# Making u\*B of three state indices with ScalarE and TensorE in a selective scan, and loading C in thirds

## The chip, the cores and the metric

The kernel runs on one core of one Trainium2 chip. The metric is the time of one execution on the device, in microseconds, median over the runs. Engines are named as in the profile: PE (TensorE, matrix products and transposes), DVE (VectorE), ACT (ScalarE), POOL (GpSimd), SP (SyncE, which only issues DMAs here).

## What is computed

One decoder layer over x of shape (4, 1024, 256) in fp32: a Mamba block, cross attention on 154 context tokens, and a mixture of four experts, each with a residual and a layer norm behind it. The change lies in the Mamba block:

```python
xz = x @ W_in.T
x_ssm, z = split(xz, 2)                        # 512 channels each
x_ssm = silu(causal_conv4(x_ssm) + conv_b)
proj = x_ssm @ W_x.T                           # B: 16, C: 16, dt: 1
dt = softplus(proj[..., -1:] * W_dt[:, 0] + b_dt)
def step(h, (dt_t, Bt, Ct, xt)):               # h: (batch, 512, 16)
    h = exp(dt_t[..., None] * A) * h + (xt * dt_t)[..., None] * Bt[:, None, :]
    y = einsum('bdn,bn->bd', h, Ct)
y = (y + x_ssm * D_param) * silu(z)
out = y @ W_out.T
```

With u = x\*dt, the term added in each step of the recurrence is u\*B of the state index n.

## The kernel before, in words

`mamba_block` (from L45) runs first, over all tokens; `attn_ffn_block` (L771) follows and isn't touched. The 4096 tokens are 16 chunks of 256 (TC), four to a batch entry. A turn i works through the 16 state indices of chunk i; beside that it prepares chunk i+1 (`prepare`), finishes the output of chunk i-1 (`finish`) and the layer norm of chunk i-2 (`settle`). Channels lie on the partitions, 512 channels as 4 groups (CT) of 128; tokens run along the free dimension.

For a state index n (a step):
- PE broadcasts row n of B to all partitions, into one of two PSUM banks `b_ps` (`b_row`, L332, run two steps ahead: PE slot n makes row n+2).
- DVE multiplies u by it, two channel groups at a time (h = 0, 1), into one of three PSUM banks `bu_ps` (`make_bu`, L677, 128x512); adds what is carried over from the chunk before to the first column (`add_carry`, L691; not in the first chunk of a batch entry); and scans (`scans`, L704, 128x512) into a ring of four `state` buffers. The order on DVE is written out in `step` (L715): make_bu(n,1), scans(n,0), add_carry(n,1), make_bu(n+1,0), scans(n,1), add_carry(n+1,0).
- ACT makes `decay` = exp(dt\*A) of step n, four instructions of 128x255, also in a ring of four, so that it can be up to four steps ahead of the scans (`step`, L482).
- POOL multiplies the state by C broadcast over the partitions (`c_bc`), 128x1024, into `state_c` (L635). A scan of step n waits for the product of step n-4.
- PE adds eight 128x128 blocks of `state_c`, transposed against the identity, to `y_ps` (`add_state`, L339, two slots behind).

All five engines run their instructions strictly in the order written here; `turn` of each engine has a list of (slot, work), and the work of slot n follows the instructions of step n. The slots of the preparation of chunk k = i+1 are, before the change: PE convolutions 0, 1, 3, 4, z tiles 5, 6, `project` 8, `step_row` 9; ACT `take_conv` 4, 7, `take_z` 8, 9, `silus` 10, `copies` 11, `terms` and `softplus` 12, `next_lead` 13; POOL `split` 8, 10, `make_dt` 10, `make_u` 11. Then come the pieces of the other chunks: PE `y_back` 11, 12 and `out_tile` 13, 14 (chunk i-1); ACT `take_sum` 0, 1, `guess` 5, `normalise` 9 (chunk i-2), `take_y_back` 14, 15 (chunk i-1); POOL `variance` 2 and `newton` 4. `take_y` on DVE stands in step 2. All matrix results of the preparation and of the output pass through one PSUM bank, `w_ps`, one after the other.

`load_c` on SP (L205) waits for `proj`, stores the rows of C of chunk k to DRAM, and loads them back broadcast over the partitions, in two halves of 8 rows; the second buffer of `c_bc` holds the other chunk. The load waits for `take_y` of the chunk that used the buffer.

Of the kernel before, what the change touches and what calls it, by code (L numbers as in the profile page):

```python
# [8 lines left out]
ALU = mybir.AluOpType  # L9
# [35 lines left out]
def mamba_block(nc, x, xT, w_in, cw, w_x, w_out, par, ident_sb, ident, sel_bc, sel_p, c_dram, x1, ahead, s_ahead):  # L45
# [7 lines left out]
    with ExitStack() as ctx:  # L53
# [8 lines left out]
        SKIP_AT = 8  # L62

# [12 lines left out]
        relu = sb("relu", [P, CT, TC])  # L76
# [48 lines left out]
        s_cb = [[sem(f"s_cb{q}{h}") for h in range(2)] for q in range(2)]  # L125
# [64 lines left out]

        block = ctx.enter_context(nc.Block())

        @block.sync
        def _(sp):
# [10 lines left out]
            def load_c(k):  # L205
# [5 lines left out]
                sp.wait_ge(s_y, count)  # L211
                for h in range(2):
                    n = NS // 2
                    sp.dma_start(c_bc[:, q, h * n:(h + 1) * n, :],
                                 c_dram[bass.ds(at(k, NS, h * n), n), :].partition_broadcast(P)).then_inc(s_cb[q][h], 16)
# [42 lines left out]
        def _(pe):  # L258
            def conv(k, j):

                q, first = k[1] % 2, k[1] % CPB == 0
                if j == 0:
                    pe.wait_ge(s_xT[q], loads(k))
                    if not is_first(k):
                        pe.wait_ge(s_abs, at(k, 2 * CT, 0))
                        pe.wait_ge(s_r, at(k, CTT, 0))
# [33 lines left out]
            def step_row(k):  # L300
                pe.wait_ge(s_projc, at(k, 2, 2))
                nc.tensor.matmul(w_ps[:, 0:TC], sel_p_sb[:, :], proj[:, k[1] % 2, :], start=True, stop=True)\
                  .then_inc(s_step, 1)

            def y_back(k, t):
                if t == 0:
                    more = k[0] is not None or k[1] + 2 < NCH
                    pe.wait_ge(s_y, at(k, 16, 48))
                    pe.wait_ge(s_abs, at(k, 2 * CT, 6 * CT) if more else 2 * CT * NCH)
                    if not more:  # L310
                        pe.wait_ge(s_r, at(k, CTT, 2 * CTT))
# [46 lines left out]
            def turn(i, prepare, finish, settle):  # L358
                k, last = shift(i, 1), shift(i, -1)
                work = []  # L360
                if prepare:
                    work += [(0, lambda: conv(k, 0)), (1, lambda: conv(k, 1)), (3, lambda: conv(k, 2)),
                             (4, lambda: conv(k, 3)), (5, lambda: z_tile(k, 0)), (6, lambda: z_tile(k, 1)),
                             (8, lambda: project(k)), (9, lambda: step_row(k))]
# [3 lines left out]
                for n in range(NS):  # L368
# [8 lines left out]
                    for place, what in work:  # L377
                        if place == n:
# [26 lines left out]
        def _(act):  # L405
# [38 lines left out]
            def terms(k, j):  # L444
                if j == 0:
# [3 lines left out]
                nc.scalar.activation(relu[:, j, :], w_ps[:, 0:TC], ACT.Relu,  # L449
                                     scale=col("W_dt", j), bias=col("b_dt", j)).then_inc(s_abs, 1)  # L450

# [1282 lines left out]
```

## Time and profile before

| | us |
|---|---|
| median of 3 runs | 1843.66 (1841.05 to 1845.77) |
| profiled execution, its time | 1843.35 |
| its span, first to last instruction | 1841.6 |
| busy PE / DVE / ACT / POOL over the span | 1483.1 / 1431.3 / 1110.4 / 919.3 |
| mean granted clock of PE | 0.895 of full |
| first and last scan (L711) start | 55.5 / 996.4 |

Busy time is the union of the intervals of an engine's instructions. Instructions of one engine overlap a little at their ends, so a pitch, from start to start, is shorter than a duration. Rows with [x <-ENGINE tile line] say that the engine stood idle for x us before the instruction and what released it.

### The profile page before, as it was taken

The numbers are of one execution on the slowest core, as the hardware profiler recorded it, in microseconds if no ns is written. First come the engines' busy times: TensorE is split into PE (matmuls) and PEld (weight loads), VectorE is DVE, ScalarE is ACT, GpSimd is POOL, SyncE is SP. The second block draws the span as 40 slices with busy tenths as digits, with TensorE's granted clock in tenths as the row PEclk, the third lists the DMA queues.
The fourth block names the chain that finished last, engine by engine and source line by source line (L and its number), as shares of the span: only waits on it lengthen the run. The fifth ranks groups of instructions, "written<-read, shape, count | busy, mean of one in ns | idle before, by whom it ended". The sixth has DMA issues, their size and how long they took to land. (4 is left out here: it accounts for less than half of the span.)

```text
span 1841.6 us, 23560 instructions
## 1 busy us (share of the span) xinstructions
PE 1483.1 (81%) x7984; PEld 1050.1 (57%) x7984; DVE 1431.3 (78%) x2667; ACT 1110.4 (60%) x2370; POOL 919.3 (50%) x758
## 2 busy tenths in 40 slices
PE   4777888777887888877866679988998899889880
PEld 3566667666776667765755345555545545464470
DVE  1899999999999999999997244395449654964578
ACT  2767877688667876787673224347634763376471
POOL 0687778877787778787785100004500460036005
PEclk9888899998898898889966879999999999999895
DMA  3311110111011110111010301000010001000000
GB/s 119 129 52 52 64 52 12 64 64 64 6 59 64 64 53 13 64 64 58 1 62 13 127 1 42 9 1 1 13 61 1 1 1 46 1 1 1 23 1 23
DMA packets 38331, 71.19 MB, mean 39 GB/s; under 512 B 3585, under 2 KB 31842, under 8 KB 33858
## 3 DMA queue, kind: packets, MB, share of 16 engines
q1 hardware_dynamic: 38210, 69.68, 11.1%
q8 instruction: 63, 1.03, 0.2%
q14 instruction: 58, 0.48, 0.1%
HBM read 61.02 MB, written 8.65 MB: 38 GB/s over the span
## 5 line engine op out<-in xcount | busy, mean ns | idle before, releaser
L635 POOL TENSOR_TENSOR state_c<-state,c_bc 128x1024 f32<-128x1024 f32 x256 | 601.5, 2361 | 127.1 <-DVE state L711 98.3
L711 DVE TENSOR_TENSOR_SCAN state<-decay,bu_ps 128x512 f32<-128x512 f32 x512 | 620.3, 1211 | 0.2 <-ACT decay L491 0.2
L491 ACT ACTIVATE decay<-dt_sb,negA 128x255 f32<-128x255 f32 x1024 | 432.4, 496 | 0.0
L686 DVE TENSOR_TENSOR bu_ps<-u_sb,b_ps 128x512 f32<-128x512 f32 x512 | 349.7, 683 | 50.6 <-POOL u_sb L556 37.4
L1330 POOL TENSOR_TENSOR big<-big,g_sb 128x1024 f32<-128x1024 f32 x29 | 79.2, 2733 | 619.0 <-ACT big L1215 617.7
L352 PE MATMUL y_ps<-ident_sb,state_c 128*128 128x128 f32 x2048 | 297.2, 293 | 18.1 <-POOL state_c L635 17.3
L352 PEld LDWEIGHTS y_ps<-ident_sb,state_c 128*128 128x128 f32 x2048 | 256.7, 152 | 53.3 <-POOL state_c L635 33.1
L273 PE MATMUL w_ps<-xT_sb,w_conv 128*128 128x256 f32 (+1 forms) x1024 | 237.1, 385 | 13.6 <-DVE w_conv L754 12.7
L273 PEld LDWEIGHTS w_ps<-xT_sb,w_conv 128*128 128x128 f32 x1024 | 193.1, 194 | 39.8 <-DVE w_conv L754 12.7
L336 PE MATMUL b_ps<-parts,sel_bc_sb 96*128 96x256 bf16 x256 | 75.7, 296 | 98.1 <-DVE bu_ps L702 74.9
L1398 DVE TENSOR_REDUCE neg<-ps 128x8 f32<-128x1232 f32 x64 | 91.0, 1436 | 69.7 <-PE ps L1009 69.7
L1129 PE MATMUL ps<-w_sb,x1T_sb 128*128 128x512 f32 x256 | 130.6, 649 | 0.0
L1164 PE MATMUL ps<-w_sb,hT 128*128 128x256 f32 x512 | 119.1, 386 | 2.4 <-ACT hT L1288 1.9
L1422 DVE BATCH_NORM_STATS2 stats<-big 128x6 f32<-128x256 f32 x256 | 88.2, 411 | 30.0 <-ACT big L1293 19.1
L412 ACT ACTIVATE xs<-w_ps,par_sb 128x256 f32<-128x256 f32 x64 | 26.8, 470 | 138.2 <-PE w_ps L273 138.2
L1164 PEld LDWEIGHTS ps<-w_sb,hT 128*128 128x128 f32 x512 | 96.0, 193 | 18.8 <-ACT hT L1288 5.1
L1273 ACT ACTIVATE big<-ps 128x1024 f32<-128x1024 f32 x32 | 32.8, 1024 | 119.5 <-PE ps L1129 119.5
L336 PEld LDWEIGHTS b_ps<-parts,sel_bc_sb 96*128 96x128 bf16 x256 | 26.2, 103 | 128.7 <-DVE bu_ps L702 93.0
L1334 POOL TENSOR_TENSOR acc<-acc,big 128x256 f32<-128x256 f32 x116 | 89.8, 774 | 9.1
L1225 ACT ACTIVATE hT<-ps 128x1024 f32<-128x1024 f32 x64 | 61.5, 1011 | 53.3 <-PE ps L1046 53.3
L1129 PEld LDWEIGHTS ps<-w_sb,x1T_sb 128*128 128x128 f32 x256 | 48.9, 205 | 52.5 <-issue 52.5
L1501 DVE COPY raw<-ps 128x512 f32<-128x512 f32 x32 | 22.1, 692 | 70.2 <-PE ps L1060 69.6
(160 smaller groups left out, 2406.6 us busy)
## 6 DMA issues: line engine op xcount, KB each, us to landing
c_bc<-c_scratch SPq DMA_DIRECT2D x32, 1024.0 KB, 5.9
res<-in_x SPq DMA_DIRECT2D x16, 256.0 KB, 2.8
x_scratch<-res SPq DMA_DIRECT2D x16, 256.0 KB, 7.5
stage<-x_scratch SPq DMA_DIRECT2D x4, 1024.0 KB, 7.1
xa<-x_scratch SPq DMA_DIRECT2D x4, 1024.0 KB, 6.2
out_x<-acc SPq DMA_DIRECT2D x4, 1024.0 KB, 4.4
xT_sb<-in_xT SPq DMA_DIRECT2D x12, 259.0 KB, 3.4
w_sb<-in_w SPq DMA_DIRECT2D x2, 1024.0 KB, 12.7
```

Of the source, the lines that this page charges most:

```text
L273: last = nc.tensor.matmul(w_ps[:, at_col + skip:at_col + TC], w_conv[:, TAPS - 1 - back, c, j * P:(j + 1) * P], xT_sb[:, q, c, HALO + skip ...
L336: nc.tensor.matmul(b_ps[n % 2][:, 0:TC], sel_bc_sb[:, n, :], parts[:, i[1] % 2, :], start=True, stop=True)\
L352: last = nc.tensor.matmul(y_ps[:, t * DI + j * P:t * DI + (j + 1) * P], state_c[:, n % RING, j, t * P:(t + 1) * P], ident_sb[:, :], start= ...
L491: nc.scalar.activation(decay[:, n % RING, j, 1:], dt_sb[:, i[1] % 2, j, 1:], ACT.Exp, scale=negA[:, j * NS + n:j * NS + n + 1]).then_inc(s ...
L635: nc.gpsimd.tensor_tensor(state_c[:, n % RING, :, :], state[:, n % RING, :, :], c_bc[:, q, n, :].unsqueeze(1).to_broadcast([P, CT, TC]), A ...
L686: nc.vector.tensor_tensor(bu_ps[m % 3][:, :].rearrange("p (j n) -> p j n", j=2), u_sb[:, i[1] % 2, 2 * h:2 * h + 2, :], b_ps[n % 2][:, 0:T ...
L711: nc.vector.tensor_tensor_scan(state[:, n % RING, pair, :].rearrange("p j n -> p (j n)"), decay[:, n % RING, pair, :].rearrange("p j n -> ...
L1129: last = nc.tensor.matmul(dst, xT[:, k, t * P:(t + 1) * P], w1_sb[:, k, h * HALF:(h + 1) * HALF], start=False, stop=k == KT - 1, skip_grou ...
L1164: last = nc.tensor.matmul(dst, hT[:, e * KT + k, i * P:(i + 1) * P], w2_sb[:, e * KT + k, :], start=False, stop=k == KT - 1, skip_group_ch ...
L1334: nc.gpsimd.tensor_tensor(acc[:, t, :], acc[:, t, :], tile[:, e * DM:(e + 1) * DM], ALU.add).then_inc(s_sum, 1)
L1398: nc.vector.tensor_reduce(neg[:, u:u + 2, :].rearrange("p m (j c) -> p j m c", c=BLK)[:, :, :, HD], ps[:, base:base + HG, 0:2 * S].rearran ...
L1422: nc.vector.bn_stats(stats[:, i * E + e, :], big[:, n, i, e * DM:(e + 1) * DM]).then_inc(s_st, 1)
```

## The change

For the state indices `OFF = (6, 10, 14)` DVE no longer makes u\*B. Instead PE transposes u to token-major (`turn_u`, 8 transposes a turn, through `w_ps`), ACT copies it to SBUF (`take_u`), and for each of the three indices ACT scales it by B, which is a per-partition scalar in that layout (`scale_u`, two activations of 128x512, each), and PE transposes the product back into PSUM (`fill`, two times four transposes), the first half into the `b_ps` bank of that index, where no row is broadcast then, the second into a `bu_ps` bank. B in token-major form comes out of `step_row` by two more transposes and is copied by `take_bT`. The Relu of `terms` goes into `u_sb` instead of a buffer of its own, and `c_bc` has three buffers of 8 rows instead of four halves; a load waits for the POOL products that read the buffer last. Slots of the preparation move: PE convolutions 2, 3, 4, 5, z 6, 7, `project` 9, `step_row` 10; ACT `take_conv` 6, 8, `take_z` 9, 10, `copies` 12, `terms`, `softplus` and `next_lead` 13; POOL's slots stay.

```diff
+        OFF = (6, 10, 14)
+        K = len(OFF)
...
-        c_bc = sb("c_bc", [P, 2, NS, TC])
+        c_bc = sb("c_bc", [P, 3, NS // 2, TC])
+        uT_sb = sb("uT_sb", [P, CTT, DI])
+        uB = sb("uB", [P, 2, CTT, DI])
+        bT = sb("bT", [P, 2, CTT, NS])
...
+        def place(i, n, h):
+            if n in OFF and h == 0:
+                return b_ps[n % 2]
+            return bu_ps[use(i, n, h) % 3]
...
-                sp.wait_ge(s_y, count)
                 for h in range(2):
...
+                    part = 2 * k[1] + h
+                    if part >= 3:
+                        sp.wait_ge(s_sc, RING + (part - 2) * n)
...
                     if not is_first(k):
-                        pe.wait_ge(s_abs, at(k, 2 * CT, 0))
-                        pe.wait_ge(s_r, at(k, CTT, 0))
+                        pe.wait_ge(s_uTc, at(k, CTT, 0))
...
+            def turn_u(i, t):
+
+                if t == 0:
+                    pe.wait_ge(s_u, at(i, 1, 1))
+                    pe.wait_ge(s_abs, at(i, 2 * CT, 2 * CT))
+                    pe.wait_ge(s_bT, at(i, 1, 1))
+                    pe.wait_ge(s_r, at(i, CTT, CTT))
+                else:
+                    pe.wait_ge(s_uTc, at(i, CTT, t))
...
+            def b_free(i, n):
...
+                before = (i, n - 2) if n >= 2 else (shift(i, -1), n - 2 + NS)
+                if before[1] in OFF:
+                    pe.wait_ge(s_scan, scanned(before[0][1], before[1], 0))
+                else:
+                    pe.wait_ge(s_bu, multiplied(*before, 1))
+
+            def fill(i, n, h):
+
+                if h == 0:
+                    b_free(i, n)
+                    pe.wait_ge(s_uB, CTT * (i[1] * K + OFF.index(n) + 1))
+                else:
+                    pe.wait_ge(s_scan, freed(i, n, 1))
+                dst, slot = place(i, n, h), (i[1] * K + OFF.index(n)) % 2
+                for e in range(2):
+                    for t in range(CTT):
+                        j = 2 * h + e
+                        last = nc.tensor.transpose(dst[:, e * TC + t * P:e * TC + (t + 1) * P],
+                                                   uB[:, slot, t, j * P:(j + 1) * P], ident_sb[:, :])
+                last.then_inc(s_fill, 1)
...
             def b_row(i, n):
+                if n in OFF:
+                    fill(i, n, 0)
+                    return
...
-                pe.wait_ge(s_bu, at(i, 4 * NS, 4 * n + 4))
+                b_free(i, n)
...
+                    if n + 1 in OFF:
+                        fill(i, n + 1, 1)
...
+            def scale_u(i, n):
+
+                o = i[1] * K + OFF.index(n)
+                act.wait_ge(s_uTc, at(i, CTT, CTT))
+                act.wait_ge(s_bT, at(i, 1, 1))
+                if o >= 2:
+                    act.wait_ge(s_fill, 2 * (o - 1))
+                for t in range(CTT):
+                    nc.scalar.activation(uB[:, o % 2, t, :], uT_sb[:, t, :], ACT.Copy,
+                                         scale=bT[:, i[1] % 2, t, n:n + 1]).then_inc(s_uB, 1)
...
+                work += [(3, lambda: take_u(i, 0)), (4, lambda: take_u(i, 1))]
                 if prepare:
...
+                    work += [(6, lambda: take_conv(k, 0)), (8, lambda: take_conv(k, 1)), (9, lambda: take_z(k, 0)),
+                             (10, lambda: take_z(k, 1)), (10, lambda: silus(k)), (12, lambda: copies(k)),
+                             (13, lambda: terms(k, 0)), (13, lambda: take_bT(k)), (13, lambda: terms(k, 1)),
+                             (13, lambda: terms(k, 2)), (13, lambda: terms(k, 3)), (13, lambda: softplus(k)),
                              (13, lambda: next_lead(k))]
+                work += [(n - 1, lambda n=n: scale_u(i, n)) for n in OFF]
...
             def make_bu(i, n, h):
 
-                m = 2 * n + h
-                if m == 0:
+                if n in OFF:
+                    return
...
+            def made(i, n, h):
+                if n in OFF:
+                    dve.wait_ge(s_fill, filled(i, n, h))
+                else:
+                    dve.wait_ge(s_bu, multiplied(i, n, h))
...
+                if more:
+                    make_bu(*following, 0)
+                    if following[1] in OFF:
+                        add_carry(*following, 0)
                 between(4 * n + 2)
                 scans(i, n, 1)
...
+                if more and following[1] not in OFF:
+                    add_carry(*following, 0)
```

## Rows read from the trace of the kernel before

**Rows 1.** Page, part 2: DVE's busy tenths in 40 slices

```profile
DVE  1899999999999999999997244395449654964578
```

**Rows 2.** Windows, turns 1-14: length, PE/PEld/DVE/ACT/POOL busy, PEclk, DMA, GB/s

```profile
110.60:940.00 829.40, 679.92 (x3777) 554.21 (x3778) 816.26 (x1289) 619.32 (x1557) 651.21 (x513) 0.90 0.14 49
```

**Rows 3.** Lines, same window: xcount | busy, mean ns | idle before, releaser

```profile
L491 ACT ACTIVATE decay<-dt_sb,negA 128x255 f32<-128x255 f32 x892 | 377.0, 496 | 0.0
...
L412 ACT ACTIVATE xs<-w_ps,par_sb 128x256 f32<-128x256 f32 x56 | 23.5, 470 | 111.7 <-PE w_ps L273 111.7
```

**Rows 4.** Timeline, DVE: start, length, engine, line, operation, tiles, xcount

```profile
110.61 1.22 DVE L711 TENSOR_TENSOR_SCAN state<-decay,bu_ps 128x512 f32<-128x512 f32 x1
...
345.00 1.21 DVE L711 TENSOR_TENSOR_SCAN state<-decay,bu_ps 128x512 f32<-128x512 f32 x1
...
353.94 1.21 DVE L669 TENSOR_TENSOR yg<-y_ps,gate 128x1024 f32<-128x1024 f32 x1
355.07 0.68 DVE L686 TENSOR_TENSOR bu_ps<-u_sb,b_ps 128x512 f32<-128x512 f32 x1
355.66 1.21 DVE L711 TENSOR_TENSOR_SCAN state<-decay,bu_ps 128x512 f32<-128x512 f32 x1
356.79 0.15 DVE L702 TENSOR_TENSOR bu_ps<-bu_ps,inject 128x2 f32<-128x2 f32 x1
356.84 0.68 DVE L686 TENSOR_TENSOR bu_ps<-u_sb,b_ps 128x512 f32<-128x512 f32 x1
357.44 1.21 DVE L711 TENSOR_TENSOR_SCAN state<-decay,bu_ps 128x512 f32<-128x512 f32 x1
...
400.04 1.21 DVE L711 TENSOR_TENSOR_SCAN state<-decay,bu_ps 128x512 f32<-128x512 f32 x1
...
403.84 1.21 DVE L711 TENSOR_TENSOR_SCAN state<-decay,bu_ps 128x512 f32<-128x512 f32 x1
...
940.02 1.21 DVE L711 TENSOR_TENSOR_SCAN state<-decay,bu_ps 128x512 f32<-128x512 f32 x1
```

**Rows 5.** Timeline of PE, turn 5

```profile
348.01 3.62 PE L273 MATMUL w_ps<-xT_sb,w_conv 128*128 128x256 f32 x16
...
364.21 3.62 PE L273 MATMUL w_ps<-xT_sb,w_conv 128*128 128x256 f32 x16
...
385.76 1.04 PE L352 MATMUL y_ps<-ident_sb,state_c 128*128 128x128 f32 x8
...
388.74 0.63 PE L315 MATMUL w_ps<-ident_sb,yg 128*128 128x128 f32 x4 [0.40 <-ACT relu L449]
...
396.68 1.97 PE L352 MATMUL y_ps<-ident_sb,state_c 128*128 128x128 f32 x8 [0.49 <-POOL state_c L635]
```

**Rows 6.** Lines, whole span, ACT: forms nearest to a scaling

```profile
L1288 ACT ACTIVATE hT<-ps,lnp_sb 128x512 f32<-128x512 f32 x64 | 45.4, 772 | 8.8 <-PE ps L1150 8.8
...
L1249 ACT ACTIVATE lnd<-lnd 128x512 f32<-128x512 f32 x32 | 20.2, 630 | 1.0
```

**Rows 7.** Part 6 of the page, DMA issues: the loads of C

```profile
c_bc<-c_scratch SPq DMA_DIRECT2D x32, 1024.0 KB, 5.9
```

**Rows 8.** Timeline of ACT, turn 5

```profile
361.07 0.20 ACT L478 ACTIVATE lnv<-var 128x2 f32<-128x2 f32 x1 [2.43 <-POOL var L603]
...
367.87 0.84 ACT L412 ACTIVATE xs<-w_ps,par_sb 128x256 f32<-128x256 f32 x2 [2.98 <-PE w_ps L273]
...
390.77 1.69 ACT L491 ACTIVATE decay<-dt_sb,negA 128x255 f32<-128x255 f32 x4
392.37 0.49 ACT L441 ACTIVATE lead<-rest,par_sb 96x256 bf16<-96x256 f32 x1
392.76 0.19 ACT L489 ACTIVATE carry<-state 128x4 f32<-128x4 f32 x1
```

**Rows 9.** Timeline of POOL, turn 5

```profile
390.85 2.36 POOL L551 TENSOR_TENSOR dt_sb<-dt_sb,relu 128x1024 f32<-128x1024 f32 x1 [2.19 <-ACT dt_sb L457]
...
394.28 2.35 POOL L635 TENSOR_TENSOR state_c<-state,c_bc 128x1024 f32<-128x1024 f32 x1
```

More of the change, by code:

```diff
@@ L62, in mamba_block @@
         SKIP_AT = 8
+        OFF = (6, 10, 14)
+        K = len(OFF)
+        USES = [(n, h) for n in range(NS) for h in range(2) if n not in OFF or h == 1]
+        PROD = [(n, h) for n in range(NS) for h in range(2) if n not in OFF]
         w_conv = sb("w_conv", [P, TAPS, KT, DI])
@@ L189, in turns, with use, scanned, freed @@
                 turn((None, r), prepare=r + 1 < NCH, finish=r >= 1, settle=r >= 2)
+        def use(i, n, h):
+            return i[1] * len(USES) + USES.index((n, h))
+        def place(i, n, h):
+            if n in OFF and h == 0:
+                return b_ps[n % 2]
+            return bu_ps[use(i, n, h) % 3]
+        def scanned(r, n, h):
+            return 2 * RING + r * 2 * NS + 2 * n + h + 1
+        def freed(i, n, h):
+            before = use(i, n, h) - 3
+            if before < 0:
+                return 0
+            return scanned(before // len(USES), *USES[before % len(USES)])
+        def multiplied(i, n, h):
+            return i[1] * len(PROD) + PROD.index((n, h)) + 1
+        def filled(i, n, h):
+            return 2 * (i[1] * K + OFF.index(n)) + h + 1
+        def broadcast(i, n):
+            return i[1] * (NS - K) + sum(m not in OFF for m in range(n + 1))
+        def added(i, n, h):
+            return (i[1] - i[1] // CPB - 1) * 2 * NS + 2 * n + h + 1
         block = ctx.enter_context(nc.Block())
@@ L376, in turn @@
                         add_state(last, NS + n - LAG)
-                    for place, what in work:
-                        if place == n:
+                    if n + 1 in OFF:
+                        fill(i, n + 1, 1)
+                    for slot, what in work:
+                        if slot == n:
                             what()
@@ L448, in terms, with take_bT, take_u @@
                                      scale=col("W_dt", j), bias=col("b_dt", j)).then_inc(s_abs, 1)
-                nc.scalar.activation(relu[:, j, :], w_ps[:, 0:TC], ACT.Relu,
+                nc.scalar.activation(u_sb[:, k[1] % 2, j, :], w_ps[:, 0:TC], ACT.Relu,
                                      scale=col("W_dt", j), bias=col("b_dt", j)).then_inc(s_abs, 1)
+            def take_bT(k):
+                if k[1] >= 2:
+                    act.wait_ge(s_uB, CTT * K * (k[1] - 1))
+                nc.scalar.activation(bT[:, k[1] % 2, :, :].rearrange("p t n -> p (t n)"),
+                                     w_ps[:, TC:TC + CTT * NS], ACT.Copy).then_inc(s_bT, 1)
+            def take_u(i, t):
+                act.wait_ge(s_uT, at(i, CTT, t + 1))
+                if t == 0 and i[1]:
+                    act.wait_ge(s_uB, CTT * K * i[1])
+                nc.scalar.activation(uT_sb[:, t, :], w_ps[:, :], ACT.Copy).then_inc(s_uTc, 1)
+            def scale_u(i, n):
[4 more added lines that the diff above has]
+                    act.wait_ge(s_fill, 2 * (o - 1))
+                for t in range(CTT):
+                    nc.scalar.activation(uB[:, o % 2, t, :], uT_sb[:, t, :], ACT.Copy,
+                                         scale=bT[:, i[1] % 2, t, n:n + 1]).then_inc(s_uB, 1)
             def softplus(k):
@@ L529, in _ @@
                 terms(first, j)
+            take_bT(first)
             softplus(first)
@@ L620, in turn @@
             def turn(i, prepare, finish, settle):
-                k, old, q = shift(i, 1), shift(i, -2), i[1] % 2
+                k, old = shift(i, 1), shift(i, -2)
                 work = []
@@ L712, in scans @@
                                              decay[:, n % RING, pair, :].rearrange("p j n -> p (j n)"),
-                                             bu_ps[m % 3][:, :], 0.0, ALU.mult, ALU.add).then_inc(s_scan, 1)
+                                             place(i, n, h)[:, :], 0.0, ALU.mult, ALU.add).then_inc(s_scan, 1)
             def step(i, n, prepare, between):
+                following = (i, n + 1) if n + 1 < NS else (shift(i, 1), 0)
+                more = n + 1 < NS or prepare
                 make_bu(i, n, 1)
```

82 lines of the change are left out of this document (44 added, 38 removed).

## The prediction

> **What bounds the kernel now.** The page comes first: VectorE (DVE) is nearly full over the first 22 of 40 slices, the Mamba stage, and half empty after it [rows 1]. The change touches only that stage. The window of its 14 middle turns (one turn is one chunk of 256 tokens) shows DVE busy for 816 of 829 us, with TensorE (PE) at 680, ScalarE (ACT) at 619 and GpSimd (POOL) at 651 [rows 2]. So DVE sets the pace and every other engine has room on average. An average hides order, however. ACT's room is time spent standing in front of a named result, 111.7 us of it for the convolutions alone [rows 3]: room that lies at a few places in the turn and is of use only there.
>
> The DVE timeline gives the pace. A step n is two scans, two products bu = u\*B and two small carry additions. Start to start, a scan takes 1.13, an addition 0.05 and a product 0.59: 3.55 a step [rows 4]. I write times as + us from a turn's first scan; turn 5 starts at 345.00 and lasts 58.8, and the 14 middle turns last (940.02 - 110.61) / 14 = 59.2 on average [rows 4]. Scan (3,1st half) starts at 357.44, +12.4.
>
> **What DVE saves.** For n = 6, 10, 14 both products go: 6 x 0.59 = 3.6 a turn. In return scan (n-1,2nd) has only small additions between itself and the addition it reads, up to 0.1 each time, 0.3 a turn (bounds 0 and 3 x 0.15). Nothing else on DVE changes. If all the rest were hidden a turn would last 55.5.
>
> **What is added elsewhere.** PE: 8 transposes of u, 24 of the scaled u, 2 small ones, less 3 row broadcasts. Four transposes take 0.63 in one group and eight add-ups with their tail 1.04 at full clock, 1.97 at the lower one [rows 5]; I take 0.5 a group of four at full clock, 1.0 at low. That is 8 x 0.5 = 4 us of PE a turn. ACT: two copies of u out of PSUM and one of B, and 6 scalings of 128x512 with a per-partition scale. No row shows that form. A 512-wide activation within SBUF with a constant scale takes 630 ns, a 512-wide one from PSUM with scale and bias from SBUF 772 [rows 6]; I take the first, which shares the memory and the width, so 1.25 a pair, and keep 1.54 as the far end. The lower end is 1.16, if one overlaps the next by 0.1, as the decays do (four at 496 ns in 1.69 [rows 3, 8]). Loads of C: each half now waits for products of an older half instead of take_y; copies(k) comes about 45 us into the turn, and store plus load (5.9 us median for the load [rows 7]) end before +60, while the first product of the next turn begins past +68. I cost it at nothing; the load of residuals behind it on SP's queue is wanted a whole turn later. The Relu going straight into u_sb costs nothing, being the same instruction. One relief: row broadcasts wait for the product alone and no more for the carry addition, 1.2 us earlier.
>
> **What is moved, and where it ends.** This decides. The preparation of the next chunk is one chain through w_ps. Today its first convolution starts at 348.01, +3.0, its last starts at 364.21 and ends at +22.8; ACT takes it at 367.87, +22.9, and after decays, silus, copies, terms and softplus begins decay(13) at 390.77, +45.8 [rows 5, 8].
>
> After the change turn_u stands first in w_ps and conv(k,0) moves to PE slot 2. There it stands behind the broadcast for step 4, which waits for product (2,2nd), done at 12.4 - 3.55 - 1.13 (take_y, 353.94 to 355.07 [rows 4]) + 0.1 = +7.8, and behind add_state(0), 0.9 more: start at about +8.9. The second pair of convolutions waits for take_conv(k,0), now in ACT slot 6, behind guess (today at 361.07, +16.1, after a wait of 2.43 for POOL's variance [rows 8]), a pair of scalings 1.25, decay(6) 1.7 and its own 0.8: +19.9. Two convolutions at 3.45, their add_states and fill(6,1) take 9.0: the last ends near +28.9, 6 us later than today.
>
> From taking that result to the end of softplus ACT needs 22.9 today, with five steps of decays in it. It needs the same afterwards, less the 0.4 that it waits today, plus scale_u(10) 1.25 and take_bT 0.25: 24.0, so softplus ends at +52.9. In the same slot 13 follow next_lead (0.4 start to start [rows 8]) and, last, scale_u(14) 1.25: +54.6. fill(14,0) on PE ends at +55.1. DVE cannot start scan (14,1st) without it. It wants it at the end of scan (13,1st): scan 13 would start at 12.4 + 10 x 3.55 - 4 x 0.59 = +45.5 with no stall, so fill(14,0) is wanted at +46.7. It is 8.4 late. Part of that shows earlier: fill(6,1) comes at +25.3 for +23.0 (2.3), and decay(11) at +42 for +40.7 (1.2); the remaining 4.9 is at step 14. Together scan (14,1st) starts at 55.1 + 0.2 + 1.13 = +56.4.
>
> Then a second wait. fill(14,1) stands behind add_state(11), and POOL makes product 11 only after make_dt, which waits for softplus: from make_dt's start to product 11 is 394.28 - 390.85 = 3.4, and product 11 takes 2.35 [rows 9]. 52.9 + 5.8 + 0.9 + 0.5 = +60.1, wanted at 56.4 + 1.13: 2.6 late. From there the turn needs its 3.55 and the 3.8 of the last step (400.04 to 403.84 [rows 4]): 56.4 + 2.6 + 7.4 = +66.4. PE stands idle for about 3 us twice before these fills; today an idle wait of that kind comes before a stretch at the lower of the two clock levels (eight transposes in 1.97 at 396.68 [rows 5]). One add_state and one fill at that level cost 0.9 more: **67.3 a turn.**
>
> **Sum.** 14 turns x (67.3 - 59.2) = +113. Turn 0 has the same chain without normalise and guess and runs 55.1 today: +7. Turn 15 prepares nothing and keeps the saving, -3.6. Rounded, +117. The profiled execution took 1843.35, 0.3 under the median of 1843.66: 1843.35 + 117 = **1960**. Low end of this case: scalings at 1.16 a pair, no low clock, product 11 not late, and 1.2 us of the relief at the broadcasts reaching conv(k,0): 62.4 a turn, +48, 1891. High end: scalings at 1.54, fills, add_states and output tiles at the lower clock (+2.5): 70 a turn, +155, 1998.
>
> **Rivals.** (a) Faster. All the added work lies in the idle time of ACT and PE, and DVE keeps its saving: 14 x (59.2 - 55.5) + 2 x 3.5 = 59 less, 1785. For it: DVE is 98% busy and ACT idle for 210 of 829 us. It decides at one point: scale_u(14) has to end by +46.2 and by my count ends at +54.6. An error of 8 us in a chain of 46 that mostly repeats rows of today would be large; 9%. A middle case within 0.3% needs the chain 7 us shorter and just so; 2%. (b) The first wait alone: the order at fill(14,1) costs nothing because product 11 is done in time. 56.4 + 7.4 = 63.8 a turn, +68 with turns 0 and 15, 1911. POOL's strict order speaks against it; 12%. (c) Transposes slower than counted. The row has eight in 1.04 us at full clock and 1.97 at low [rows 5]. If every added group and the add_states beside it run at the low level, the path gains 0.5 for each of four groups and 0.9 for each of two add_states on top: 3.8 - 0.9 already counted = 2.9 a turn, +44, 2004; 4%, as PE stands at 0.90 of full clock over these turns [rows 2], most of them spent at the higher level. The Trainium skill (TensorE: Matmul & The Clock Gate, Part 4: PE-mode transpose) says a transpose took about 275 ns in a kernel and doesn't count as activity that keeps the clock at full. By that figure, an estimate, 34 transposes would cost 9 us of PE a turn in place of 4; eight in 1.04 us here disagree with the duration, and no row separates the clock part. My forecast holds 73%.
>
> **Numbers.** Cases (my forecast, b, c and part of the uncertainty of each) are slower: 89%. A measurement of this kernel tells 0.3%, 5.5 us, from no change. The range 1890 to 2000 holds the forecast's ends and (b).
>
> **What the new profile should show.** DVE busy in the middle turns near 85%, down from 98%, with idle before the carry addition L702 and the scan L711, released by PE's fills; some ACT-released idle at step 11. Mean turn near 67. ACT's scalings of about 0.63, the third pair ending near +54.6, directly after next_lead. conv(k,0) near +9. POOL waits longer for softplus. I am wrong if conv(k,0) starts before +5 or the third pair of scalings ends before +47, and the later stages should not move at all.

## The result, and the profile after

The changed kernel takes 1973.97 us in the median (1971.84 to 1977.89, 4 runs) against 1843.68 for the kernel before: a ratio of 1.071, 95% interval 1.0687 to 1.0733. Slower by 130 us, where 1960 was forecast.

The page after:

```profile
span 1976.1 us, 24624 instructions
...
PE 1561.1 (79%) x8480; PEld 1119.7 (57%) x8480; DVE 1383.0 (70%) x2571; ACT 1185.0 (60%) x2514; POOL 919.5 (47%) x758
...
DVE  1778888787878778787878915448555855674578
```

DVE lost 48 us of work (1431.3 to 1383.0) and the span grew by 134.5. Its row of tenths, full through the Mamba stage in [rows 1], now has sevens and eights in it. Where the time lies can be read from the first scans of the turns: 16 numbers from the trace of either kernel.

| | before | after | difference |
|---|---|---|---|
| start of the first scan | 55.5 | 58.6 | +3.1 |
| turn 0 | 55.1 | 64.6 | +9.5 |
| turns 1 to 14, mean of one | 59.24 | 68.21 | 14 x 8.97 = +125.6 |
| first to last scan of turn 15 | 56.3 | 53.0 | -3.3 |
| last scan to the end | 845.2 | 845.0 | -0.2 |

The windows view over the same 14 turns (length, then busy PE, PEld, DVE, ACT, POOL, clock, DMA) answers to [rows 2]:

```profile
123.20:1078.00 954.80, 752.32 (x4210) 619.02 (x4209) 774.32 (x1205) 684.78 (x1683) 650.48 (x512) 0.88 0.12 42
```

DVE falls from 98% to 81% of its turns. No engine has taken its place: PE is at 79%, ACT at 72%, POOL at 68%. So this is a chain of waits and not a full engine. The waits view of the same stretch (total us, times, longest) names its links:

```profile
POOL rest L699 <- ACT lead L524: 114.0, 14, 8.4
...
DVE b_ps L827 <- PE b_ps L386: 67.3, 22, 5.1
DVE bu_ps L827 <- PE bu_ps L386: 60.8, 22, 3.3
...
PE y_ps L442 <- DVE yg L788: 28.1, 14, 2.0
DVE state L838 <- ACT decay L606: 27.8, 17, 4.3
```

DVE stands 128 us for fills (L386), which did not exist before, and 28 us for ACT's decay. The timeline of DVE in turn 5, which now runs from 394.51 to 463.42, 68.9 us (columns as in [rows 4], the idle time and its releaser in brackets), gives each of them its place:

```profile
394.51 1.21 DVE L838 TENSOR_TENSOR_SCAN state<-decay,bu_ps 128x512 f32<-128x512 f32 x1
...
412.24 0.69 DVE L806 TENSOR_TENSOR bu_ps<-u_sb,b_ps 128x512 f32<-128x512 f32 x1 [0.36 <-PE b_ps L426]
...
417.01 0.17 DVE L827 TENSOR_TENSOR b_ps<-b_ps,inject 128x2 f32<-128x2 f32 x1 [1.11 <-PE b_ps L386]
...
422.77 0.17 DVE L827 TENSOR_TENSOR bu_ps<-bu_ps,inject 128x2 f32<-128x2 f32 x1 [3.35 <-PE bu_ps L386]
...
439.37 1.22 DVE L838 TENSOR_TENSOR_SCAN state<-decay,bu_ps 128x512 f32<-128x512 f32 x1 [0.97 <-ACT decay L606]
...
452.82 0.17 DVE L827 TENSOR_TENSOR b_ps<-b_ps,inject 128x2 f32<-128x2 f32 x1 [5.06 <-PE b_ps L386]
...
457.42 0.17 DVE L827 TENSOR_TENSOR bu_ps<-bu_ps,inject 128x2 f32<-128x2 f32 x1 [2.19 <-PE bu_ps L386]
...
463.42 1.21 DVE L838 TENSOR_TENSOR_SCAN state<-decay,bu_ps 128x512 f32<-128x512 f32 x1
```

These are the first halves and second halves of index 6 (417.01, 422.77) and of index 14 (452.82, 457.42); for index 10 DVE doesn't wait. 439.37 is the scan of step 11, behind ACT. Together with 0.36 us before the product at 412.24 this is 13.0 us of idle time in the turn. Minus the 3.6 that DVE saves it gives 9.4 of the 10.1 us by which turn 5 grew. The addition at 452.82 stands ahead of the second scan of step 13, which reads nothing of the fill and waits behind it all the same; the order with that scan (1.13 us) first was not tried.

### The profile page after: what moved, and what is told of

Same layout as the page of the kernel before. It is cut to its first block and busy times, and to the rows that moved or that the text cites. A ratio compares the mean times of both kernels' runs of the same rounds, so it can differ in the third digit from the quotient of the medians.

```text
span 1976.1 us, 24624 instructions
## 1 busy us (share of the span) xinstructions
PE 1561.1 (79%) x8480; PEld 1119.7 (57%) x8480; DVE 1383.0 (70%) x2571; ACT 1185.0 (60%) x2514; POOL 919.5 (47%) x758
## 5 line engine op out<-in xcount | busy, mean ns | idle before, releaser
L838 DVE TENSOR_TENSOR_SCAN state<-decay,bu_ps 128x512 f32<-128x512 f32 x464 | 561.5, 1212 | 26.6 <-ACT decay L606 16.1
L442 PE MATMUL y_ps<-ident_sb,state_c 128*128 128x128 f32 x2048 | 314.8, 305 | 94.4 <-POOL state_c L754 64.2
L442 PEld LDWEIGHTS y_ps<-ident_sb,state_c 128*128 128x128 f32 x2048 | 266.3, 158 | 130.0 <-POOL state_c L754 83.3
L806 DVE TENSOR_TENSOR bu_ps<-u_sb,b_ps 128x512 f32<-128x512 f32 x416 | 284.4, 684 | 60.9 <-POOL u_sb L674 40.0
L316 PE MATMUL w_ps<-xT_sb,w_conv 128*128 128x256 f32 (+1 forms) x1024 | 258.2, 410 | 13.6 <-DVE w_conv L880 12.6
L316 PEld LDWEIGHTS w_ps<-xT_sb,w_conv 128*128 128x128 f32 x1024 | 209.4, 210 | 45.7 <-DVE w_conv L880 12.6
L426 PE MATMUL b_ps<-parts,sel_bc_sb 96*128 96x256 bf16 x208 | 58.6, 283 | 57.7 <-DVE bu_ps L806 48.0
L827 DVE TENSOR_TENSOR bu_ps<-bu_ps,inject 128x2 f32<-128x2 f32 x348 | 52.4, 150 | 60.8 <-PE bu_ps L386 60.8
L699 POOL TENSOR_TENSOR rest<-proj,lead 96x256 f32<-96x256 f32 x16 | 10.7, 668 | 164.7 <-ACT lead L524 164.7
```

Source lines behind the costliest of these rows:

```text
L316: last = nc.tensor.matmul(w_ps[:, at_col + skip:at_col + TC], w_conv[:, TAPS - 1 - back, c, j * P:(j + 1) * P], xT_sb[:, q, c, HALO + skip ...
L442: last = nc.tensor.matmul(y_ps[:, t * DI + j * P:t * DI + (j + 1) * P], state_c[:, n % RING, j, t * P:(t + 1) * P], ident_sb[:, :], start= ...
L806: nc.vector.tensor_tensor(place(i, n, h)[:, :].rearrange("p (j n) -> p j n", j=2), u_sb[:, i[1] % 2, 2 * h:2 * h + 2, :], b_ps[n % 2][:, 0 ...
L838: nc.vector.tensor_tensor_scan(state[:, n % RING, pair, :].rearrange("p j n -> p (j n)"), decay[:, n % RING, pair, :].rearrange("p j n -> ...
```

## What the chain looks like now

PE in turn 5 (answers to [rows 5]):

```profile
404.83 1.97 PE L442 MATMUL y_ps<-ident_sb,state_c 128*128 128x128 f32 x8 [2.02 <-DVE yg L788]
406.59 5.51 PE L316 MATMUL w_ps<-xT_sb,w_conv 128*128 128x256 f32 x16
...
412.92 3.62 PE L316 MATMUL w_ps<-xT_sb,w_conv 128*128 128x256 f32 x16
...
422.57 3.62 PE L316 MATMUL w_ps<-xT_sb,w_conv 128*128 128x256 f32 x16
...
451.69 1.09 PE L386 MATMUL b_ps<-ident_sb,uB 128*128 128x128 f32 x4 [2.76 <-ACT uB L564]
...
455.85 1.09 PE L442 MATMUL y_ps<-ident_sb,state_c 128*128 128x128 f32 x8 [0.61 <-POOL state_c L754]
456.78 0.60 PE L386 MATMUL bu_ps<-ident_sb,uB 128*128 128x128 f32 x4
```

The first convolution starts at 406.59, +12.1 from the turn's first scan, where it was +3.0. It stands behind add_state(0), which waited 2.02 us for DVE's take_y (the waits view has this 14 times, 28.1 us), and after that idle time both run at the lower clock (granted clock 0.50 from 403.57 to 410.39): the add_state in 1.97 us where 1.04 is usual, the convolution in 5.51 us where the next takes 3.62. The last convolution ends near 426.0.

ACT in the same turn (answers to [rows 8]):

```profile
410.67 0.20 ACT L593 ACTIVATE lnv<-var 128x2 f32<-128x2 f32 x1 [6.88 <-POOL var L721]
...
416.58 0.84 ACT L504 ACTIVATE xs<-w_ps,par_sb 128x256 f32<-128x256 f32 x2 [2.55 <-PE w_ps L316]
...
426.23 0.84 ACT L504 ACTIVATE xs<-w_ps,par_sb 128x256 f32<-128x256 f32 x2 [5.43 <-PE w_ps L316]
...
448.87 1.06 ACT L572 ACTIVATE dt_sb<-dt_sb 128x1024 f32<-128x1024 f32 x1
449.83 0.49 ACT L533 ACTIVATE lead<-rest,par_sb 96x256 bf16<-96x256 f32 x1
450.23 1.32 ACT L564 ACTIVATE uB<-uT_sb,bT 128x512 f32<-128x512 f32 x2
```

The second take_conv is at 426.23, +31.7, against +22.9 before. Softplus (448.87) ends at +55.4, next_lead follows at 449.83, and only then the two scalings for index 14 (450.23, 1.32 us the pair), which end at +57.0. PE's fill of index 14 starts at 451.69 after 2.76 us of waiting for them, at the lower clock (1.09), and DVE goes on at 452.82. The second fill (456.78) stands behind the add_state at 455.85, which waits for POOL:

```profile
442.43 0.67 POOL L699 TENSOR_TENSOR rest<-proj,lead 96x256 f32<-96x256 f32 x1 [8.16 <-ACT lead L524]
...
450.00 2.35 POOL L669 TENSOR_TENSOR dt_sb<-dt_sb,u_sb 128x1024 f32<-128x1024 f32 x1 [2.28 <-ACT dt_sb L572]
...
453.43 2.36 POOL L754 TENSOR_TENSOR state_c<-state,c_bc 128x1024 f32<-128x1024 f32 x1
```

Product 11 (453.43) comes 3.43 us after make_dt starts (450.00), as before the change. POOL's wait for softplus has not grown (2.28); it waits one piece of work earlier, for `lead` out of ACT's copies, 8.16 us in this turn.

## The experiments

Two theories stood at first. **A:** the preparation of the next chunk is one chain that ends in the fills, u and the row broadcast of the next turn; it now starts later, and the turn lasts as long as it does. **B:** the added work itself (scalings, transposes, fills) and the 5 us wait for the first fill of index 14 set the turn. Ratios are to runs of the kernel before on the same chip; the turn is the mean of turns 1 to 14.

**Scaling ahead of copies and terms.**

```diff
-                work += [(n - 1, lambda n=n: scale_u(i, n)) for n in OFF]
+                work += [(n - 1 if n < 14 else 11, lambda n=n: scale_u(i, n)) for n in OFF]
```

> Edit: the scaling for index 14 moves from the end of ScalarE's slot 13 to slot 11, ahead of copies and terms. Theory A (the late preparation chain sets the turn; its last link is fill(14,1) behind product 11, which waits for softplus): fill(14,0) comes about 1.6 us earlier, but softplus and with it product 11 and fill(14,1) come 1.3 us later, so the wait at step 14 shrinks and the next one grows: a turn of 69.0 to 69.8 in place of 68.2 to 68.9, 1974 goes to 1985 to 1995. Theory B (the 5.06 us wait for fill(14,0), behind softplus and the scaling, is what costs): it goes, 3 to 5 us a turn less, 1905 to 1930.

Measured: 2015.83 us, ratio 1.0868 (1.0848 to 1.0888), 70.75 a turn. DVE's timeline in turn 5, the additions of index 14:

```profile
461.40 0.17 DVE L827 TENSOR_TENSOR b_ps<-b_ps,inject 128x2 f32<-128x2 f32 x1 [2.46 <-PE b_ps L386]
...
470.28 0.17 DVE L827 TENSOR_TENSOR bu_ps<-bu_ps,inject 128x2 f32<-128x2 f32 x1 [6.12 <-PE bu_ps L386]
```

The wait that looked most costly fell from 5.06 to 2.46 us, and the kernel became slower (70.75 us a turn against 68.21). What shrank at the first half came back at the second, 6.12 for 2.19, since softplus and so product 11 lie behind the moved scaling. Theory B is out as far as it ranks that wait first. A had the direction and too small a size (69.0 to 69.8): the second fill now runs at the lower clock as well.

**Fill ahead of add_state.**

```diff
+                    if n + 1 in OFF:
+                        fill(i, n + 1, 1)
                     if n >= LAG:
                         add_state(i, n - LAG)
                     elif finish:
                         add_state(last, NS + n - LAG)
-                    if n + 1 in OFF:
-                        fill(i, n + 1, 1)
```

> Edit: in each slot TensorE issues fill(n,1) ahead of add_state instead of behind it, so that fill(14,1) no longer waits for product 11. Theory A: fill(14,1) then follows y_back(1), about 1.8 us earlier than now, and fill(6,1) 0.9 earlier (which changes nothing, since the later wait absorbs it): a turn 1.5 to 1.8 us shorter, 1945 to 1952. Theory B (the wait at step 14 for the first fill sets the turn and the second is only its echo): within 5 us of 1974.

Measured: 1965.21 us, ratio 1.0596 (1.0574 to 1.0617), 67.07 a turn. On the first chip's scale that is 1.0596 x 1843.68 = 1954, 2 us above A's range and far from B's; the turn gained 1.1 us where 1.5 to 1.8 were expected. In turn 5 the wait at the second half of index 14 fell from 2.19 to 0.35, and 0.9 came back as a wait for the next turn's row broadcast.

**No index made by ScalarE and TensorE, with the new and with the old slots.** Both leave out turn_u, take_u, scale_u and the fills; the slots are all that stands between them.

```diff
-        OFF = (6, 10, 14)
+        OFF = ()
...
-                work += [(n - 1, lambda n=n: scale_u(i, n)) for n in OFF]
```

> Edit: no index is made by ScalarE and TensorE (OFF is empty, so VectorE makes all 16 products; no transposes of u, no scalings, no fills), with all the rest of the change, its later slots of the preparation included. Theory A: the slots alone make most of the loss: convolutions start near +12, softplus ends near +54, u and the broadcast for the next turn come near +63, a turn of 64 to 66, 1915 to 1945. Theory B (the added transposes and scalings cost the time): about the time of the kernel before, 1838 to 1855.

Measured: 1957.57 us, ratio 1.0564 (1.0548 to 1.058), 66.87 a turn, 0.9 above A's range. B is out.

> Edit: as the run with no index and new slots, but with the preparation in the slots of the kernel before, so that only the side edits are left: C in thirds, Relu into u, B transposed in step_row and copied, row broadcasts that wait for the product and not for the carry addition. Both theories: 1835 to 1850. If it is above 1860, one of the side edits has a cost that neither has counted.

Measured: 1833.06 us, ratio 0.9894 (0.9877 to 0.991), 58.56 a turn, 2 us under the range.

This pair carries the verdict. Without one scaling or fill, the slots alone take the turn from 58.56 to 66.87: +8.3 us, of the 9.0 by which it grew in all. The added work and the saving on DVE together are worth the 1.3 us between 66.87 and 68.21. And the side edits, left alone, are a gain of 1%, which no theory had. (The three indices were not run in the old slots, so that what they cost there is not shown.)

With no fill to wait for, DVE's idle time comes at the row broadcasts, the next turn's first among them. The waits view from 115 to 1010 us, with the new slots:

```profile
DVE bu_ps L803 <- PE b_ps L427: 60.1, 65, 5.0
...
DVE bu_ps L803 <- issue: 44.8, 12, 5.0
```

With the old slots it has only the second of the two:

```profile
DVE bu_ps L803 <- issue: 5.0, 6, 2.0
```

In turn 5 with the new slots (first scan at 384.34) PE and DVE show how that wait ends:

```profile
444.54 1.97 PE L443 MATMUL y_ps<-ident_sb,state_c 128*128 128x128 f32 x8 [1.95 <-POOL state_c L751]
446.30 2.89 PE L412 MATMUL w_ps<-w_out_sb,y_sb 128*128 128x256 f32 x8
...
449.45 0.27 PE L427 MATMUL b_ps<-parts,sel_bc_sb 96*128 96x256 bf16 x1
```

```profile
449.82 0.70 DVE L803 TENSOR_TENSOR bu_ps<-u_sb,b_ps 128x512 f32<-128x512 f32 x1 [3.54 <-issue]
```

The profile names no releaser for the 3.54 us ("issue"), but the product starts 0.1 us after the broadcast at 449.45 is done, and this stands behind an add_state that waits for POOL and an output tile at the lower clock.

**One half of the slots each.** Index list empty again; in the first only ACT's entries of the preparation are the late ones, in the second only PE's.

```diff
-                    work += [(2, lambda: conv(k, 0)), (3, lambda: conv(k, 1)), (4, lambda: conv(k, 2)),
+                    work += [(0, lambda: conv(k, 0)), (1, lambda: conv(k, 1)), (3, lambda: conv(k, 2)),
...
```

> Edit: as the run with no index and old slots, but ScalarE's part of the preparation in the later slots of the change (TensorE's stays in the old ones). Theory A (any link of the preparation chain that is moved later delays the next turn's u and broadcast): take_conv(k,0) then stands behind guess (+16), the third convolution starts near +19 in place of +15, softplus ends near +50; a turn of 61 to 63 in place of 58.6, 1865 to 1895. Theory B (TensorE's later start is all of it, ScalarE only follows): 1833 to 1845.

Measured: 1940.06 us, ratio 1.0504 (1.0479 to 1.053), 66.04 a turn: more than A allowed. In turn 5, which starts at 372.35, ACT's timeline shows guess after 7.37 us of waiting for POOL's variance, and the second take_conv late:

```profile
388.43 0.20 ACT L592 ACTIVATE lnv<-var 128x2 f32<-128x2 f32 x1 [7.37 <-POOL var L718]
...
402.28 0.84 ACT L505 ACTIVATE xs<-w_ps,par_sb 128x256 f32<-128x256 f32 x2 [7.62 <-PE w_ps L318]
```

and PE's the third convolution, which had to wait for the first take_conv, which stands behind guess:

```profile
379.17 3.62 PE L318 MATMUL w_ps<-xT_sb,w_conv 128*128 128x256 f32 x16
...
391.33 6.47 PE L318 MATMUL w_ps<-xT_sb,w_conv 128*128 128x256 f32 x16 [5.24 <-ACT xs L505]
```

After 5.24 us of waiting the convolution takes 6.47 us in place of 3.62. The expectation had the wait (the third convolution starts at +19.0, as it said) and not the clock behind it. Turn 1 is a control inside the run: it has no chunk i-2 and so no guess, and lasts 59.2 us, turns 2 to 14 66.1 to 66.9. One entry, moved from slot 4 to 6, puts the chain behind work of another chunk.

> Edit: the other half: TensorE's part of the preparation in the later slots, ScalarE's in the old ones. Theory A: the first convolution starts near +11 to +12 (behind the broadcast for step 4 and an add_state that waits for take_y), ScalarE stands in slots 4 and 7 for it, softplus ends near +51 to +52; a turn of 63 to 66, 1890 to 1935. Theory B: the whole loss, 1950 to 1960.

Measured: 1963.33 us, ratio 1.063 (1.0607 to 1.0654), 67.28 a turn. That is above A's range, and 3 us above B's: B, that TensorE's half alone makes the whole loss, was the nearer one here. Either half alone costs nearly what both cost together (66.04, 67.28, 66.87), so the halves don't add. The two halves don't lose the time at the same place, though. With ACT late, DVE waits over the middle turns 80.3 us for row broadcasts and 23.6 without a named releaser, as with all slots late. With PE late it waits 97.8 us for ACT's decays: in turn 5 it waits 3.21 us at +22.8, behind ACT's 14.93 us in its early slot for the first convolutions, and 3.62 at +55.0, behind terms and softplus.

**The start of the convolutions, in the changed kernel.**

```diff
-                    work += [(2, lambda: conv(k, 0)), (3, lambda: conv(k, 1)), (4, lambda: conv(k, 2)),
+                    work += [(1, lambda: conv(k, 0)), (2, lambda: conv(k, 1)), (4, lambda: conv(k, 2)),
```

> Edit: the changed kernel, with the first two convolutions one slot earlier on TensorE (1 and 2 in place of 2 and 3), nothing else. The first one starts near +7.5 in place of +12.1, at full clock; but the second pair still waits for take_conv behind guess (+16), so the last convolution ends 2 to 2.5 us earlier. Theory A (the turn follows the end of the convolutions one to one): a turn of 65.7 to 66.3 in place of 68.2, 1938 to 1950. Theory B (the fills and scalings set the turn wherever the convolutions stand): within 6 us of 1974.

Measured: 1945.31 us, ratio 1.0548 (1.053 to 1.0565), 65.94 a turn: as A said.

```diff
-                    work += [(0, lambda: take_sum(old, 0)), (1, lambda: take_sum(old, 1)), (5, lambda: guess(old)),
-                             (9, lambda: normalise(old))]
+                    work += [(0, lambda: take_sum(old, 0)), (1, lambda: take_sum(old, 1)), (9, lambda: normalise(old))]
...
-                    work += [(6, lambda: take_conv(k, 0)), (8, lambda: take_conv(k, 1)), (9, lambda: take_z(k, 0)),
+                    work += [(6, lambda: take_conv(k, 0)), (6, lambda: settle and guess(old)), (8, lambda: take_conv(k, 1)), (9, lambda: take_z(k, 0)),
```

> Edit: as the run with the first convolutions one slot earlier, and guess moved from slot 5 to behind take_conv in slot 6, so that the scaling for index 6 and take_conv no longer stand behind POOL's variance. Theory A: the second pair starts near +17 and the last convolution ends 5 to 6.5 us earlier than in the changed kernel: a turn of 62 to 63.5, 1885 to 1912, still slower than the kernel before. Theory B: as the run before it, or within 6 us of 1974.

Measured: 1905.75 us, ratio 1.0338 (1.0322 to 1.0353), 63.25 a turn. Turn 5 starts at 377.12, and ACT takes the convolutions at +15.9 and +26.6:

```profile
393.03 0.84 ACT L504 ACTIVATE xs<-w_ps,par_sb 128x256 f32<-128x256 f32 x2 [2.09 <-PE w_ps L316]
...
403.67 0.84 ACT L504 ACTIVATE xs<-w_ps,par_sb 128x256 f32<-128x256 f32 x2 [5.63 <-PE w_ps L316]
```

With all scalings and fills in place, moving three entries (two convolutions and guess) gave back half of the loss. How far the turn follows the chain can be read off two numbers, from turn 5 of each run (the runs with a reordering and with one count are described below):

| run | second take_conv | turn | rest |
|---|---|---|---|
| before | +22.9 | 58.8 | 36.0 |
| earlier convolutions and guess | +26.6 | 64.1 | 37.5 |
| earlier convolutions | +28.8 | 66.9 | 38.0 |
| no index, ACT late | +29.9 | 66.3 | 36.4 |
| no index, PE late | +30.1 | 66.5 | 36.4 |
| no index, all late | +31.3 | 67.9 | 36.6 |
| the change, fill first | +31.0 | 66.5 | 35.5 |
| the change | +31.7 | 68.9 | 37.2 |
| no index, old slots | +21.7 | 58.6 | 36.9 |
| scaling ahead of copies | +31.5 | 71.3 | 39.8 |
| no index, reordered | +21.7 | 58.6 | 36.9 |
| two indices, reordered | +21.7 | 62.0 | 40.3 |
| two indices, fill first | +23.5 | 57.9 | 34.4 |
| kernel before, one count | +21.7 | 58.8 | 37.1 |

In the first eight rows the rest of the turn behind that point is 35.5 to 38.0 us, whether three indices or none are made elsewhere; that is what theory A says. In the rows with the old slots and no index DVE is full as well, and their sum proves nothing. The rest is not a constant: it was 39.8 and 40.3 in two runs in which the second fill of index 14 came late (6.12 and 5.23 us of waiting), and 34.4 where two indices are made elsewhere and no fill is late.

**A version that keeps the chain where it was.** First a control: no index, old slots, and the output of chunk i-1 out of `w_ps` a slot earlier.

```diff
-                    work += [(14, lambda: take_y_back(last, 0)), (15, lambda: take_y_back(last, 1))]
+                    work += [(13, lambda: take_y_back(last, 0)), (14, lambda: take_y_back(last, 1)),
+                             (15, lambda: take_sum(last, 0))]
...
+                    ahead_of += [(13, lambda: out_tile(last, 0)), (14, lambda: out_tile(last, 1))]
```

> Edit: as the run with no index and old slots, and besides the output of chunk i-1 leaves w_ps earlier: take_y_back in slots 13, 14 in place of 14, 15, take_sum in 15 and 0 in place of 0 and 1, out_tile ahead of add_state in its slot. VectorE makes all products. Theory A: the chain gains 1 to 2 us of room at the turn's end, but VectorE at 58.5 us a turn is the bound already, so the time stays: 1828 to 1836. Rival: the reordering alone shortens a turn, under 1825.

Measured: 1832.87 us, ratio 0.9927 (0.9908 to 0.9946), 58.28 a turn. DVE is the bound, as expected: it is busy for 813.5 of the 815.9 us of the middle turns. Then two indices on top, with the transposes of u ahead of the convolutions' old slots and the scalings where ACT was idle:

```diff
+        OFF = (8, 14)
...
+                work, ahead_of = [], [(0, lambda: turn_u(i, 1))]
+                    ahead_of.append((15, lambda: turn_u(k, 0)))
...
+                work += [(1, lambda: take_u(i, 0)), (2, lambda: take_u(i, 1))]
+                work = [(3, lambda: scale_u(i, 8)), (4, lambda: scale_u(i, 14))]
```

> Edit: the same reordering with two indices, 8 and 14, made by ScalarE and TensorE. u is transposed in TensorE's slots 15 and 0, ahead of the convolutions that keep their old slots, and the two scalings stand in ScalarE's slots 3 and 4, where it waits for a convolution. Theory A (the method pays where it adds nothing to the preparation chain): VectorE needs 2.4 us less, the chain is 0.5 longer and cuts some of it: a turn of 57.1 to 57.6, 1810 to 1822. Theory B (the added transposes and scalings cost more than the product on VectorE): above 1833.

Measured: 1876.66 us, ratio 1.0168 (1.0148 to 1.0188), 61.39 a turn. Theory A was wrong, and the time lies in B's range. PE's timeline, turn 6 (first scans at 421.9 and 483.6; columns as before):

```profile
471.31 3.78 PE L411 MATMUL w_ps<-w_out_sb,y_sb 128*128 128x256 f32 x8 [1.16 <-ACT y_sb L582]
474.88 1.06 PE L416 MATMUL w_ps<-res,ident_sb 128*128 128x256 f32 x2
475.74 1.34 PE L442 MATMUL y_ps<-ident_sb,state_c 128*128 128x128 f32 x8
476.91 0.60 PE L386 MATMUL bu_ps<-ident_sb,uB 128*128 128x128 f32 x4
```

and DVE's, the addition that waits for it:

```profile
477.55 0.17 DVE L832 TENSOR_TENSOR bu_ps<-bu_ps,inject 128x2 f32<-128x2 f32 x1 [5.23 <-PE bu_ps L386]
```

The reordering had put out_tile (471.31, at the lower clock 3.78 + 1.06 us) ahead of the second fill of index 14 (476.91): 5.2 us of DVE a turn, from an order that costs nothing without fills. Fill and row broadcast of the next turn ahead of it:

```diff
+                    if n + 1 in OFF:
+                        fill(i, n + 1, 1)
+                    if n == 13 and prepare:
+                        b_row(k, 0)
```

> Edit: as the run with two indices and the reordering, but fill(n,1) goes ahead of out_tile and add_state in its slot, and the broadcast of the next turn's row 0 goes from slot 14 to slot 13, right behind it. In the run before, DVE stood 5.2 us for fill(14,1), which TensorE issued behind out_tile. Theory A (a fill or broadcast behind an instruction that waits for the end of the preparation chain is what costs): the wait goes, a turn of 57.0 to 58.5 in place of 61.4, 1808 to 1832, and so no slower than the run with no index. Theory B (the two indices cost more than they save): 1850 or more.

Measured: 1834.55 us, ratio 0.9948 (0.9933 to 0.9962), 58.38 a turn: within A's range for the turn, 2.6 us above its range for the time. The loss is gone, and so is any gain: DVE does 1.9 us less a turn (busy for 786.8 us of the middle turns) and the turn is no shorter than the 58.28 of the control. The idle time has come back in small waits: over the middle turns 11.1 us for broadcasts, 13.1 ahead of take_y, whose releaser the profile doesn't name, and 4.0 for `inject`. Nor did this version keep the chain where the control has it. In the mean of the middle turns the rest behind the second take_conv is 2.2 us shorter than in the control (34.4 for 36.6), which is about what DVE saves, and the second take_conv comes 2.3 us later (+24.0 for +21.6): in turn 5 the first convolution stands behind turn_u and starts at +5.4, in the control at +2.9. The saving is there, and the later start takes it. Whether some order of PE's work has the one without the other was not found.

**The one per cent of the side edits.**

```diff
-                pe.wait_ge(s_bu, at(i, 4 * NS, 4 * n + 4))
+                pe.wait_ge(s_bu, at(i, 4 * NS, 4 * n + 3))
```

> Edit: the kernel before, with one number changed: a row broadcast waits for the product that read its bank last and not for the carry addition behind the scan that follows (a count of 4n+3 in place of 4n+4). Theory A (the 1% that the side edits gain is this relief at the turn's end, where VectorE waited for the broadcast 12 times): VectorE's wait for b_ps falls under 3 us in the middle turns, a turn of 58.5 to 58.8 in place of 59.2, ratio 0.988 to 0.996. Rival (the gain is the loads of C or another side edit): ratio 0.997 to 1.002.

Measured: 1837.39 us, ratio 0.9962 (0.9949 to 0.9976), 58.62 a turn. DVE's wait for broadcasts in the middle turns, from the waits view:

```profile
DVE bu_ps L686 <- PE b_ps L336: 3.5, 4, 1.6
```

It was 12.3 us in 12 waits. A's range for the turn holds; the wait is 0.5 us above what it said and the ratio 0.0002 above its range, and the interval touches the rival's 0.997. In the traces this one count makes up nearly all of the difference between the kernel before and the run with no index and old slots (59.24, 58.62 and 58.56 a turn). The intervals of the two ratios, 0.9962 and 0.9894, don't meet, but they were taken on chips on which the kernel before took 1845.0 and 1853.3 us. Whether the rest is the chip or another side edit stays open: they did not run on one chip. The run with no index and old slots has the lowest ratio of all, 0.9894; the others below 1 are 0.9927 (reordered), 0.9948 (two indices, fill first) and 0.9962, each from another chip, so that their order is not shown. The one of them that makes u\*B elsewhere shows no profit over its own control.

## Why the prediction was right

The forecast of 1960 was 14 us low, by the mechanism that it named, a chain of waits that the later slots lengthen. By its own steps:

- **What bounds the kernel now, and the room of ACT and PE.** Right. ACT's and PE's idle time lay ahead of named results and was of no use.
- **What DVE saves.** Turn 15, which prepares nothing, lost 3.3 us for the 3.6 of the sum.
- **First convolution at +8.9.** Measured +12.1. The step counted the broadcast and missed that add_state(0) waits for take_y, and that PE then runs at the lower clock: 0.9 in the add_state, 1.9 in the convolution. Part of it was absorbed, because take_conv stood behind guess anyway: the last convolution ended at +31.5 for +28.9.
- **From take_conv to the end of softplus, 24.0.** Measured 23.7 (+31.7 to +55.4). This, the longest term, was read off a row of the kernel before.
- **Scaling at 1.25 a pair.** 1.32; one takes 709 ns, between the bounds of 630 and 772. The Trainium skill (ScalarE: Activation LUTs, What ACT_TABLE_LOAD costs) states for one activation 186 ns, 93 more for each per-partition operand, and 0.833 ns an element: an estimate of 705 ns for 512 elements with one such operand, and the trace agrees.
- **The four waits 2.3, 1.2, 4.9, 2.6.** Measured 4.5 (two halves of index 6), 1.0, 5.1, 2.2.
- **67.3 a turn.** 68.2. The profiled execution took 1977.89, 17.9 us above the forecast and 3.9 above the median, and 12.7 of these 17.9 lie in the 14 middle turns. That the mean is so near is in part luck: in turn 5, 68.9 us long, softplus ended 2.5 us later than counted and the first scan of step 14 started 3.1 later (+59.5 for +56.4), and only 1.6 of this reached the turn's end, since 0.9 for the lower clock stood in the sum behind that point and the second wait was 0.4 shorter. The first terms that were too small are the start of the first convolution and the wait for the second fill of index 6.
- **Turn 0 and the start.** +9.5 for +7, and the start, not in the sum, was 3.1 later: `project` took 3.70 us there for 1.94. The fill-first run has the same code up to there and starts its scans at 55.3, so that this is the clock and not the change.
- **POOL waits longer for softplus.** Wrong: 31.9 us for 30.9 over the middle turns. POOL had fallen behind one piece earlier, at `split`, 114 us for 30.4.
- **DVE busy near 85%.** 81%.

Rival (a) wanted the third pair of scalings to end by +46.2; it ended at +57.0. Rival (b) fell with the timeline, where product 11 is late as counted (a wait of 2.19 us for the 2.6 of the sum); taking the second fill out from behind it gained 1.1 us a turn. Of rival (c), a fill of four transposes takes 0.60 us at the higher clock and 1.09 at the lower, as the rows above have it. In the tile view of `bu_ps` from 400 to 470 us one transpose lasts 272 ns in the median (twelve of them). The Trainium skill (TensorE: Matmul & The Clock Gate, Part 4: PE-mode transpose) gives about 275 ns for one, and the trace agrees. The prediction said that the rows disagree with it, and that was a misreading: transposes of a group overlap, so that four end after 0.60 us and not after 1.09. Whether transposes keep the clock up less than matmuls was not tried.

What the forecast did not separate, and the pair with the empty index list did: the slots, which the change moved to make room for turn_u in `w_ps`, cost 8.3 us a turn by themselves, the side edits give back 0.7, and the added work, less what DVE saves, costs 1.3, together the 9.0 measured.

## What to carry to other kernels

When a busy engine is relieved with work for idle ones, write down where their idle time lies and what ends it, and walk the chain that passes through it: here an engine at 98% and a chain of the same length stood side by side, and to start the chain 9 us later cost 8 us a turn. Moving the entries of one engine alone, TensorE's or ScalarE's, cost nearly as much. The largest wait in a profile need not be the one that counts: cutting the 5.06 us wait in half made the kernel about 1.5% slower (1.0868 against 1.071, each against the kernel before on its own chip), because its remedy stood in the way of the next link. And look at which event a wait asks for: one count, 4n+3 for 4n+4, gained 0.4%, where the whole change lost 7%.

## What was not expected of the hardware

A wait of PE can cost more than its length, since PE was often at the lower of its two clock levels behind it. After 2.02 us of idle time in one turn and 5.24 in another (granted clock 0.50 at the start of what followed) the next convolution took 5.51 and 6.47 us for 3.62. A chain that leaves PE idle just ahead of its own longest piece then pays for the wait and again for the piece: in the run with ACT's late slots that is 2.9 of the 4.3 us by which turn 5 (66.3) exceeded the middle of its expected range. It is not so after every wait. In the last run with two indices PE stood idle for 2.77 us, and the four transposes behind it took 0.66 us at granted clock 1.00; the clock fell 2.1 us later. The DVE scan reads its input as fast from `b_ps` (1.19 us) as from `bu_ps` (1.21).
